# An attention and mixture-of-experts block on one core: scores in pairs of array strips, the maximum as ScalarE's bias, and a moved order

## The reference

```
# per layer: x (16,128,512), ctx (16,128,256), 32 heads of 16
q = (layernorm(x) @ Wq); k, v = split(ctx @ Wkv)
q, k = apply_axial_rope(q, pos), apply_axial_rope(k, pos)
logits = einsum('bqhd,bkhd->bhqk', q, k) * scale        # scale = 1/sqrt(16)
w = softmax(logits, axis=-1)
x = x + tanh(g_xattn) * (einsum('bhqk,bkhd->bqhd', w, v) @ Wout + bout)
xf = layernorm(x)                                        # 2048 tokens
probs = softmax(xf @ gate_w.T); routing_weights, selected = top_k(probs, 6)   # of 16 experts
moe_out = sum over selected of weight * (silu(g) * u) @ w2,  g, u = xf @ w1.T
x = x + tanh(g_ffn) * (moe_out + shared_out)
```

## Time and profile before

| | us |
|---|---|
| three runs, median (lowest to highest) | 1501.24 (1496.4 to 1513.0) |
| the profiled execution | 1500.2 |
| its span, first to last instruction | 1498.0 |
| phase A, first 16 batches' rounds, then to the first block of phase B | 0 to 567 |
| starts of the first score of batches 2 and 15 | 98.1 and 496.7 |

### The profile page before, as it was taken

One profiled execution on the slowest core, in us unless ns is written; L12 is line 12 of the kernel. 1 busy time (PEld: TensorE's weight loads), 2 busy tenths in 40 slices (PEclk: granted clock), 3 DMA queues, 4 the chain that ended last, 5 costly groups with the idle time before them and its releaser, 6 DMA issues.

```text
span 1498.0 us, 32482 instructions
## 1 busy us (share of the span) xinstructions
PE 1408.3 (94%) x8414; PEld 1187.6 (79%) x8415; DVE 839.9 (56%) x1682; ACT 499.7 (33%) x982; POOL 700.7 (47%) x1135
## 2 busy tenths in 40 slices
PE   4899999999999955999999999999999999999998
PEld 2566666666666644899999999999999999898987
DVE  4677777778777743444444444444444444256666
ACT  3344444445444411233333333333333333111111
POOL 3457754444544241548354555555555400745553
PEclk8799999999999856999999999999999999999999
DMA  5022323211321225534444444444443442356674
GB/s 190 18 92 76 134 92 134 75 75 75 119 105 65 79 108 178 168 100 141 144 141 144 141 144 141 143 143 143 143 143 107 122 143 86 104 166 202 206 206 138
DMA packets 146857, 190.03 MB, mean 127 GB/s; under 512 B 32531, under 2 KB 99604, under 8 KB 144116
## 3 DMA queue, kind: packets, MB, share of 16 engines
q1 hardware_dynamic: 125108, 99.31, 22.3%
q0 software_dynamic: 21696, 90.06, 17.5%
HBM read 116.80 MB, written 72.50 MB: 126 GB/s over the span
## 4 chain that ended last, share of the span: by engine, by line
PE 73%; DVE 13%; issue 5%; ACT 3%; SPq 2%; POOL 1%; DMA 1%; DVEq 0%; ACTq 0%; POOLq 0%
PE bank L1362 33%; PE bank L1396 18%; PE bank L616 8%; PE bank L641 5%; DVE smax L888 3%; PE bank L1373 3%; PE bank L654 2%; DVE soft L891 2%; PE bank L623 2%; PE bank L671 1%; ACT soft_t L533 1%; SPq L1183 1%; DVE x L937 1%; ACT soft L527 1%; DVE stats L940 1%
## 5 line engine op out<-in xcount | busy, mean ns | idle before, releaser
L1362 PE MATMUL bank<-w_hi,x_hi 128*128 (+1 forms) x1144 | 289.6, 334 | 21.0 <-DVE x_lo L1437 18.5
L1362 PE MATMUL bank<-w_hi,x_lo 128*128 (+1 forms) x1144 | 277.2, 323 | 0.0
L1362 PE MATMUL bank<-w_lo,x_hi 128*128 (+1 forms) x1144 | 276.9, 323 | 0.0
L205 POOL CAST w_hi<-w_raw 128x352 fp32r<-128x352 f32 x144 | 69.2, 531 | 379.2 <-PE bank L1362 379.2
L1453 DVE SCALAR_TENSOR_TENSOR act<-silu,row_w,bank 128x352 f32<-128x352 f32 x111 | 64.4, 580 | 301.2 <-ACT silu L1311 300.3
L1362 PEld LDWEIGHTS bank<-w_hi,x_hi 128*128 128x128 f32 x1144 | 193.0, 190 | 21.3 <-issue 18.6
L1311 ACT ACTIVATE silu<-bank 128x352 f32<-128x352 f32 x143 | 66.5, 465 | 402.7 <-PE bank L1362 402.7
L1362 PEld LDWEIGHTS bank<-w_lo,x_hi 128*128 128x128 f32 x1144 | 200.2, 189 | 0.0
L1362 PEld LDWEIGHTS bank<-w_hi,x_lo 128*128 128x128 f32 x1144 | 199.6, 189 | 0.0
L1396 PE MATMUL bank<-w_hi,a_hi 128*128 (+3 forms) x429 | 171.4, 400 | 7.6 <-DVE a_lo L1441 6.9
L1396 PE MATMUL bank<-w_lo,a_hi 128*128 (+3 forms) x429 | 169.7, 396 | 0.0
(11 more groups left out here) (183 smaller groups left out, 2316.8 us busy)
## 6 DMA issues: line engine op xcount, KB each, us to landing
xr<-expert_rows SPq DMA_DIRECT2D x444, 64.0 KB, 1.9
y_rows<-y SPq DMA_DIRECT2D x111, 256.0 KB, 2.0
w_raw<-in_w POOLq DMA_DIRECT2D x18, 1408.0 KB, 6.7
w_raw<-in_w POOLq DMA_DIRECT2D x18, 512.0 KB, 7.8
x_sb<-in_x SPq DMA_DIRECT2D x16, 256.0 KB, 3.0
x_res<-in_x SPq DMA_DIRECT2D x16, 256.0 KB, 3.9
x_rows<-x SPq DMA_DIRECT2D x16, 256.0 KB, 4.3
x_rows<-row SPq DMA_DIRECT2D x16, 256.0 KB, 4.4
```

Of the source, the lines that this page charges most:

```text
L205: nc.gpsimd.tensor_copy(w1_hi[d][half][:, s], w1_raw[:, d, halves[half]]).then_inc(w_hi_made, 1)
L1362: last = nc.tensor.matmul(to[:, 0:WIDTH], xx[jt][:, d, :], w[d][half][:, cols], start=(d == 0 and xx is x_hi and w is w1_hi), stop=(d == D ...
```

## The change

- **Scores in pairs.** `score_pair` runs at even u and issues the eight instructions of groups u and u + 1, group u, group u + 1, group u, group u + 1, by two instructions. The two groups lie on different strips of 32 array rows and in different banks. The pair waits until the exponential of group u - 1 has ended.
- **The maximum as a bias.** The maximum is written negated, and the subtraction is gone. The exponential reads the score bank itself, in four instructions of 128 elements a row, each with one column of the maximum as bias. The scale moves into the two masks with which ACT copies the keys.
- **Order.** q transposes go from group 4 to 3, k transposes from 5 to 4, with ACT's copies. The row transposes and `x2_hi` go from the end of TAIL's round to group 0 of PLACE's, `c_hi` and `c_lo` from LOAD's group 7 to PROJECT's groups 0 and 1. The out projection is cut in two halves of six matmuls, one at the end of group 3 and one after the pair of group 4; its reader on DVE goes from group 4 to 5. The gate's chain goes from group 5 to 3, LOAD's statistics from 2 to 3 and its normalised rows from 6 to 7, TAIL's from 6 to 7. `rank` also waits for DVE's reader of the out projection. SP starts x's load ahead of the wait for `c_lo`.

```diff
-                    r = 32 * (u % 4)
-                    need(pe, shifted, b * GROUPS + u - 1)
+                    need(pe, exp_done, b * GROUPS + u)
                     for c in range(2):
-                        ch = 2 * (u // 4) + c
-                        last = nc.tensor.matmul(bank[2 + u % 2][:, c * 2 * P:(c + 1) * 2 * P],
-                                                q_t[j][r:r + 32, ch, :],
-                                                k_t[j][r:r + 32, ch].rearrange("p e n -> p (e n)"),
-                                                start=True, stop=True)
-                    last.then_inc(score_mm, 1)
+                        for w in (u, u + 1):
+                            r, ch = 32 * (w % 4), 2 * (w // 4) + c
+                            last = nc.tensor.matmul(bank[2 + w % 2][:, c * 2 * P:(c + 1) * 2 * P],
+                                                    q_t[j][r:r + 32, ch, :],
+                                                    k_t[j][r:r + 32, ch].rearrange("p e n -> p (e n)"),
+                                                    start=True, stop=True)
+                            if c == 1:
+                                last.then_inc(score_mm, 1)
...
-                    act.wait_ge(shifted, b * GROUPS + u + 1)
-                    a.activation(soft[u % 2][:], soft[u % 2][:], ACT.Exp, scale=SCALE).then_inc(exp_done, 1)
+                    act.wait_ge(smax_done, b * GROUPS + u + 1)
+                    need(act, prob_mm, b * GROUPS + u - 1)
+                    for h in range(4):
+                        last = a.activation(soft[u % 2][:, h, :], bank[2 + u % 2][:, h * P:(h + 1) * P], ACT.Exp,
+                                            bias=smax[u % 2][:, h:h + 1])
+                    last.then_inc(exp_done, 1)
...
-                v.tensor_reduce(smax[u % 2][:], s3, AX.X, ALU.max).then_inc(smax_done, 1)
-                dve.wait_ge(smax_done, b * GROUPS + u + 1)
-                need(dve, prob_mm, b * GROUPS + u - 1)
-                v.tensor_tensor(soft[u % 2][:], s3, smax[u % 2][:, :, None].to_broadcast([P, 4, P]), ALU.subtract)\
-                    .then_inc(shifted, 1)
+                v.tensor_reduce(smax[u % 2][:], s3, AX.X, ALU.max, negate=True).then_inc(smax_done, 1)
```

More of the change, by code:

```diff
@@ L563, in one_round @@
                     attend(at, u)
-                    if at(PROJECT) and u == 5:
+                    if at(PLACE) and u == 0:
+                        b = at(PLACE)[0]
+                        act.wait_ge(x2_mm, b + 1)
+                        need(act, gate_mm, b)
+                        a.activation(x2_hi[:].rearrange("p c n -> p (c n)"), bank[1][:], ACT.Copy)\
+                            .then_inc(x2_hi_done, 1)
+                    if at(PROJECT) and u == 0:
+                        b = at(PROJECT)[0]
+                        act.wait_ge(c_in, 16 * (b + 1))
+                        need(act, v_mm, b)
+                        a.activation(c_hi[:], c_raw[:], ACT.Copy).then_inc(c_hi_done, 1)
+                    if at(PROJECT) and u == 4:
                         b, j, n = at(PROJECT)
@@ L588, in one_round @@
                         split_weights("q")
-                    if at(LOAD) and u == 7:
-                        b, j, n = at(LOAD)
-                        act.wait_ge(c_in, 16 * (b + 1))
-                        need(act, v_mm, b)
-                        need(act, c_lo_done, b)
-                        a.activation(c_hi[:], c_raw[:], ACT.Copy).then_inc(c_hi_done, 1)
-                    if at(TAIL) and u == 7:
-                        b = at(TAIL)[0]
-                        act.wait_ge(x2_mm, b + 1)
-                        need(act, gate_mm, b)
-                        a.activation(x2_hi[:].rearrange("p c n -> p (c n)"), bank[1][:], ACT.Copy)\
-                            .then_inc(x2_hi_done, 1)
                     if at(PLACE) and u == 2:
@@ L628, in _, with score_pair @@
             pe.wait_ge(ones_done, 2)
-            def scores(at, u):
+            def score_pair(at, u):
                 if at(ATTEND):
@@ L717, in transpose_values, with project_out @@
                 four_transposes(bank[1], attn[:].rearrange("p h d -> p (h d)")).then_inc(at_mm, 1)
-            def project_out(b, j, n):
-                if isinstance(b, int) and b == 0:
-                    pe.wait_ge(w_lo_done, 3)
-                pe.wait_ge(at_lo_done, b + 1)
-                three(bank[1][:], at_parts, o_w, DC, lambda t, c: t[:, c, :], lambda w, c: w[:, c, :])\
-                    .then_inc(o_mm, 1)
+            def project_out(half, b, j, n):
+                if half == 0:
+                    if isinstance(b, int) and b == 0:
+                        pe.wait_ge(w_lo_done, 3)
+                    pe.wait_ge(at_lo_done, b + 1)
+                for c in (2 * half, 2 * half + 1):
+                    for l, r in ((0, 0), (0, 1), (1, 0)):
+                        last = nc.tensor.matmul(bank[1][:], at_parts[l][:, c, :], o_w[r][:, c, :],
+                                                start=(c == 0 and l == 0 and r == 0), stop=(c == DC - 1 and l == 1))
+                if half == 1:
+                    last.then_inc(o_mm, 1)
             def transpose_row(b, j, n):
@@ L858, in load @@
                 if u == 7:
-                    dve.wait_ge(c_hi_done, b + 1)
-                    need(dve, v_mm, b)
-                    v.tensor_tensor(c_lo[:], c_raw[:], c_hi[:].bitcast(F32), ALU.subtract).then_inc(c_lo_done, 1)
-                if u == 6:
                     dve.wait_ge(var1, b + 1)
@@ L876, in project @@
                 if u == 1:
+                    dve.wait_ge(c_hi_done, b + 1)
+                    v.tensor_tensor(c_lo[:], c_raw[:], c_hi[:].bitcast(F32), ALU.subtract).then_inc(c_lo_done, 1)
                     dve.wait_ge(q_mm, b + 1)
```

67 lines of the change are left out of this document (34 added, 33 removed).

## The result

| | before | after |
|---|---|---|
| median of the runs, us | 1507.06 (1496.4 to 1513.0, 18 runs) | 1495.21 (1482.25 to 1505.72, 18 runs) |
| profiled execution, us | 1500.2 | 1482.25 |
| its span and mean granted clock | 1498.0, 0.964 | 1480.4, 0.955 |

The ratio is 0.9924, with a 95% interval of 0.9902 to 0.9945: a gain of 0.8%, where 1.5% was forecast.

The account below looks back on a forecast made before the run. TensorE bounds phase A (29.5 us work, 1.2 us waits a round). From 1500.2 us: full rounds -29.4, clock +16, first two batches -4, batch 15 -4, together -21.4: 1478 us, own range 1468 to 1488, with rivals 1457 to 1497.

Parts of the forecast that it names:

- the scores in pairs: TensorE's scores: two row strips run at once, a pair takes 1.06 us, saving 4.2 us a round.
- rival 3: The row strips don't overlap: a pair costs 2.1 us, a round 32.3, time about 1520 us; chance 0.12.
- The maximum as a bias: ScalarE's four short exponentials take 1.2 us (bounds 1.0 to 1.5); VectorE loses 5.5 us of subtractions a round.
- rival 2: ScalarE's four short exponentials take 1.5 to 1.6 us, a round 29.9, time 1496 us; chance 0.18.
- The new chain: A full round walked through the queues: 28.4 us, 25.0 of work and 3.3 of waits; -29.4 us over 13 rounds.
- The edges: Outside the 13 full rounds: first two attended batches -4 us, batch 15's round -4 us.
- The clock: TensorE's clock falls in 10 of 13 full rounds (bounds 0 and 13), 1.6 us each: +16 us.
- the wait of 1.8 us where there was none over 0.7: TensorE's forecast wait ahead of the pair of groups 6 and 7, given as evidence against the clock holding.
- Moved parts cost nothing else: The moved `c_hi`, `c_lo`, `x2_hi`, `x2_lo` and `rank`'s added wait fit their new places at no cost.
- POOL's order is unchanged: GpSimd's queue keeps its order; its second norm ends near 26.3 us, VectorE's row behind it starts at 26.8.
- rival 1: The clock holds because shorter pairs keep TensorE dense: the +16 us goes, time 1462 us; chance 0.22.
- The fourth: Something unseen in the order, a wait across engines at the rounds' end: 1488 to 1505 us; chance 0.05.

Follow-up runs that it names:

- e_clo_back: The changed kernel with only `c_hi` and `c_lo` back at the end of LOAD's round; 1495.94 us, ratio 0.9926.
- e_clo_fill: The changed kernel with group 4's transposes run four times and `c_hi` and `c_lo` back at the end of LOAD's round; 1464.30 us, ratio 0.9739.
- e_fill3: The changed kernel with group 4's transposes run four times instead of once; 1465.14 us, ratio 0.9760.
- e_bias_only: The kernel before with only the maximum as the exponential's bias, scores single and in the old places; 1499.27 us, ratio 0.9965.
- e_late_fill: The changed kernel with expert 1's weights split in later rounds and group 4's transposes run four times; 1454.72 us, ratio 0.9676.

## Why the prediction was wrong, point by point

**What bounded the kernel, and the scores in pairs:** right. A pair takes 1.06 us, as said, and rival 3 (no overlap) is out. **The maximum as a bias:** right. Four exponentials take 1.15 us against 1.2, so rival 2 is out, and that its 1496 is so near the measured 1495 is luck; the estimate from the slope between 16 and 512 elements held for 128. **The new chain:** right. At full clock the waits are 0.94 to 1.03, 0, about 0.2 and 1.60 us against 1.0, 0.1, 0.4 and 1.8, the maximum of group 4 stands behind the statistics, and a round at full clock is 28.1 us against 28.4. That part alone made 13 x (30.66 - 28.1) = 33 us.

**The edges:** too small. Ahead of the full rounds and behind them the profiled execution gained 15.5 us where 8 were put: 3.1 in batches 0 and 1 (4 were put), 7.7 behind the full rounds (4 were put), and 2.9 ahead of the first score and 1.8 in phase B, where nothing was put. Most of the 2.9 comes with the place of `c_hi` and `c_lo`: with them back, the first score is at 32.9 and 33.0 us in e_clo_back and e_clo_fill, with them moved at 30.6. The rest was not followed further.

**The clock, first step that failed:** the count was nearly right, the price was not. In the profiled execution nine of 13 rounds have a fall, ten were forecast, and the mean granted clock is 0.93 where 0.9 was said. But the price of 1.6 us came from one fall of 3.4 us. Most falls here last 6.8 us and cost 30.98 - 28.1 = 2.9 us (mean of the five such rounds that nothing else disturbed); those of 3.4 us cost 1.2. In the profiled execution the clock's term in the 11 rounds without the split is 16.9 us, as it happens the 16 of the sum. At the median it is far more. The 18 runs of the changed kernel have mean clocks from 0.955 (1482.25 us) to 0.929 (1505.72 us), and a line through them gives 8.0 us per 0.01. The median's clock is 0.94, and e_fill3, at 0.97, is 25 to 30 us faster. The term of +16 should have been 25 to 30. What I overlooked is that a fall's length varies. Nor is a fall bound to the sign that I read, "the wait of 1.8 us where there was none over 0.7": in e_bias_only ten of 13 rounds have one, without a wait that its profile shows. What makes the clock fall stays open; shown is what holds it. The Trainium skill ("TensorE: Matmul & The Clock Gate", Part 1: The HAM clock gate) says that the same kernel can meet the gate at another phase from run to run; the spread of 23.5 us, against 4.7 where the clock holds, agrees. One profiled execution is then a sample of the clock's loss, not its median.

**"Moved parts cost nothing else", second step that failed:** `c_hi` and `c_lo` "lie under the q projection" was reckoned with the durations of a quiet round, not against what else runs at the new place in each round. GpSimd's split of expert 1's weights, 10.5 us in one piece, was in the trace of before, at 134.2 us. At the old place `c_lo` ran ahead of it, beside GpSimd's scatter. At the new place it ran into it and took 10.7 us. The Trainium skill ("SBUF — State Buffer", Who interferes with whom) has the rule: a VectorE instruction with both inputs in SBUF contends with a GpSimd instruction that reads SBUF. `c_lo` has both in SBUF, and the trace agrees; in the kernel before, the subtractions that ran beside the split (134.2 to 144.8 us) read a PSUM bank and kept their 0.67 to 0.69 us. I had priced the row and not asked for its neighbours. "POOL's order is unchanged" was true and beside the point: its queue stayed, but the reader of its rotation moved 6 us up in the round, into the time of the split. Cost: 14 us in the two rounds of the profiled execution with their falls, 10.4 at full clock.

**The rivals:** rival 1 (the clock holds, 1462) is not what happened, but e_fill3 brings it about and gives 1465. The fourth, a wait across engines that I don't see, had 0.05, and it is about half of the answer. The measured 1495 lies within the 1457 to 1497 of the prediction, but near the end that was meant for rival 2, whose mechanism did not happen; that too is luck.

The sum with the measured terms, against the three runs' 1501: -33 for the rounds, -15.5 for the edges, +10.4 for the split, +30 for the clock give 1493 (1488 with 25 for the clock). The median of the changed kernel is 1495. By the 18 runs of the kernel before (1507) the gain is 11.9 us where this sum has 8.4; what remains is within what the medians of one kernel differ from set to set (1499.9 to 1507.1 for the kernel before). The edges are those of two profiled executions and the clock's term that of the medians, so the sum is a rough one.

## What to carry to other kernels

When an instruction is moved, look in every round, also those with one-off work, at what the neighbouring engines do at its new place: a two-input VectorE instruction beside a long GpSimd run is held, and a reader that moves up needs its producers moved up too. Where TensorE is the bound, work or waits taken out of it can cost it its clock, so price a fall by its length and look at the mean clock of several runs, of the old kernel as well as of the new. An order with projections between the light groups held the clock here, and with the late split it was worth more than the change. If one disturbance hides another, hold the first still: with the clock held, 10 us could be read that drowned without it.

## What the runs showed of the hardware

- **VectorE was held across a run of GpSimd instructions.** `c_lo` waited not for one instruction of 0.4 to 0.9 us but for all 16, 10.7 us. A much smaller one, `prob` (L971 of e_clo_fill, 128 x 16 elements), took 2.27 us where it otherwise takes 0.23: it began in the split and ended at 138.04 us, as the first instruction of the rotation behind it ended (138.00). In e_late_fill it took 2.37 us beside the late split and ended with it (472.93 against 472.89).
- **Row strips overlap whole.** Eight instructions on two strips of 32 rows take 1.06 us in turn and 1.07 in a row, as long as four on one strip.
- **The clock falls without an idle TensorE.** In e_bias_only TensorE was busy for 26.28 of 26.35 us up to 430.7 us, where the clock went from 1.00 to 0.50. In the changed kernel repeated transposes held it at 0.99 to 1.00, added 16-column matmuls only in part (0.95), with the same wait left ahead of the pair.
